# Second attention of a vision tower: in four of six score rounds, two products with the same keys become one of 392 columns

## The reference, cut to what matters

```
q = layernorm(x @ Wq.T per head) ; k = layernorm(x @ Wk.T per head) ; v = x @ Wv.T
scores = einsum('bqhs,bkhs->bhqk', q, k) / sqrt(16), causal
out = einsum('bhqk,bkhs->bqhs', softmax(scores), v) @ Wo.T + bo
```

## Time and profile before

| | us |
|---|---|
| runs | 1964.82, 1959.18, 1961.18 |
| median | 1961.18 |
| span of the profiled execution | 1907.7 |
| median less that span | 53.5 |
| TensorE busy in the span | 1666.0 (87%) |
| VectorE, ScalarE, GpSimd busy | 1201.1, 1076.6, 1162.9 |

### The profile page before, as it was taken

One profiled execution on the slowest core, in us unless ns is written; L12 is line 12 of the kernel. 1 busy time (PEld: TensorE's weight loads), 2 busy tenths in 40 slices (PEclk: granted clock), 3 DMA queues, 4 the chain that ended last, 5 costly groups with the idle time before them and its releaser, 6 DMA issues. The chain is left out here.

```text
span 1907.7 us, 45923 instructions
## 1 busy us (share of the span) xinstructions
PE 1666.0 (87%) x13765; PEld 1251.6 (66%) x13766; DVE 1201.1 (63%) x4836; ACT 1076.6 (56%) x2574; POOL 1162.9 (61%) x1108
## 2 busy tenths in 40 slices
PE   4999999995569764699999999999994999999996
PEld 2666666663447543467667677676662999998995
DVE  2899999983743002678888888888864343433442
ACT  2666666651436432467776776777751555555553
POOL 2455655531057885226776766767656687878876
PEclk8999999995569887699999999999997999999998
DMA  8989999931014433311111111211112455545553
GB/s 198 237 209 222 216 223 234 228 97 52 12 40 78 67 53 60 106 32 48 53 53 51 53 55 46 58 51 53 41 45 62 66 71 65 69 68 65 72 67 40
DMA packets 257801, 172.48 MB, mean 90 GB/s; under 512 B 25598, under 2 KB 250656, under 8 KB 257632
## 3 DMA queue, kind: packets, MB, share of 16 engines
q1 hardware_dynamic: 206432, 134.16, 28.9%
q0 software_dynamic: 50112, 35.64, 13.8%
q10 hardware_dynamic: 1088, 0.53, 0.2%
HBM read 117.64 MB, written 52.40 MB: 89 GB/s over the span
## 5 line engine op out<-in xcount | busy, mean ns | idle before, releaser
L2373 POOL DMA_INDIRECT out_dram<-r_yw,r_idx x212 | 332.5, 1568 | 94.2 <-issue 41.4
L2255 POOL DMA_INDIRECT rows_scratch<-routed_row,slot_u x256 | 254.2, 993 | 169.8 <-DVE slot_u L2194 106.7
L2438 ACT ACTIVATE r_hT<-r_p_up,r_b1T 128x256 f32<-128x256 f32 x424 | 191.6, 474 | 123.4 <-PE r_p_up L2413 120.0
L1920 ACT ACTIVATE a_probsT<-a_p_sc 98x392 f32<-98x392 f32 x384 | 170.7, 501 | 109.7 <-PE a_p_sc L1677 72.0
L2401 PEld LDWEIGHTS r_p_y<-w_all,r_hT 128*128 128x128 f32 x1696 | 224.1, 193 | 11.1
L2413 PE MATMUL r_p_up<-r_xgT,r_w1e 128*128 128x256 f32 x848 | 222.4, 386 | 9.3 <-DVE r_w1e L2453 8.7
L2401 PE MATMUL r_p_y<-w_all,r_hT 128*128 x1696 | 224.8, 276 | 0.0
L449 PE MATMUL p_embed<-pix,w_pix 96*128 96x392 f32 x512 | 209.2, 516 | 3.5 <-ACT pix L568 3.5
L2025 DVE TENSOR_REDUCE a_negmax<-a_p_max 98x2 bf16<-98x392 f32 x256 | 132.5, 559 | 61.4 <-PE a_p_max L1642 61.4
L718 POOL TENSOR_SCALAR vare<-mv 98x4 f32<-98x4 f32 x64 | 29.9, 467 | 218.3 <-DVE mv L703 199.5
L2413 PEld LDWEIGHTS r_p_up<-r_xgT,r_w1e 128*128 128x128 f32 x848 | 147.1, 194 | 22.5 <-issue 8.0
(11 more groups left out here) (377 smaller groups left out, 4171.6 us busy)
## 6 DMA issues: line engine op xcount, KB each, us to landing
img<-in_x_dram SPq DMA_DIRECT2D x192, 196.0 KB, 4.3
img<-in_x_dram SPq DMA_DIRECT2D x192, 189.0 KB, 4.5
r_xg<-rows_scratch SPq DMA_DIRECT2D x106, 130.0 KB
xn_scratch<-xn SPq DMA_DIRECT2D x32, 196.0 KB
h_scratch<-h SPq DMA_DIRECT2D x32, 196.0 KB
h<-h_scratch SPq DMA_DIRECT2D x32, 196.0 KB
h3b<-h_scratch SPq DMA_DIRECT2D x32, 196.0 KB
out_dram<-h SPq DMA_DIRECT2D x32, 196.0 KB
```

The source lines that it names most:

```text
L1920: act.activation(probsT[:, u % 2, i, :], p_sc[i % 2][:, 0:2 * PAIR], ACT.Exp).then_inc(exped, 1)
L2255: pool.indirect_dma_start(rows_dram, bass.IndirectOffsetOnAxis(ap=slot_u[:, u % ROWS, c, t:t + 1], axis=0), row[:, u % ROWS, c, t, :], Non ...
L2373: pool.indirect_dma_start(acc_dram, bass.IndirectOffsetOnAxis(ap=idx[:, (k - 3) % 4, t:t + 1], axis=0), yw[:, (k - 3) % 4, t, :], None, co ...
L2438: act.activation(hT[:, (k - 1) % 2, f, :], p_up[f][:, 0:G], ACT.Silu, bias=b1T[:, bass.ds(e * FC + f, 1)]).then_inc(act_h, 1)
```

## The change

Where the bank's two products have the same keys, the x = 0 turn makes both in one instruction pair of 392 columns: the moving operand is variant 0 and variant 1 of the same queries (two stretches of 196 columns, 392 elements apart), the output the whole bank as (x, c). The x = 1 turn makes nothing in these rounds. The rounds with m None are as before.

```diff
                                           q_var[rows, s4, var:var + 2, o:o + TILE], start=(x == 0), stop=False,
                                           skip_group_check=True)
-                            else:
+                            elif x == 0:
                                 o = m * PAIR
-                                pe.matmul(p_sc[p][:, x * PAIR:(x + 1) * PAIR], kT[rows, s4, o:o + TILE],
-                                          q_var[rows, s4, var + x, o:o + PAIR], start=(x == 0), stop=False,
-                                          skip_group_check=True)
+                                pe.matmul(p_sc[p][:, 0:LIVE * PAIR].rearrange("p (x c) -> p x c", x=LIVE),
+                                          kT[rows, s4, o:o + TILE], q_var[rows, s4, var:var + LIVE, o:o + PAIR],
+                                          start=True, stop=False, skip_group_check=True)
```

## The result

The changed kernel takes 1937.70 us (median of six runs, 1931.91 to 1942.93), the kernel before, with three more runs beside it, 1958.22 us (1953.33 to 1964.82). Ratio 0.9893, 95% interval 0.9872 to 0.9915: 20.5 us less, where 1.1 were forecast.

What follows compares the result with a forecast made beforehand. TensorE's streaming of columns was taken to bound the second attention; 0.8 us from the stream plus 0.3 us from stalls made 1.1 us less, 1961.18 to 1960.1 us, range 1956.5 to 1964.5.

Steps and rivals of the forecast that it cites:

- The median and the span: Whole kernel: runs' median is 53.5 us above the trace's span of 1907.7 and takes the same 1.1 us difference.
- two signs that were named for a wrong prediction: 392-column pass not 0.329 us, or a stage outside 780 to 1450 us differing by more than a clock stretch.
- Streams: Score passes: columns stay, two passes of 392 replace four of 196; 6 ns gained a round, 0.8 us in all.
- Weight loads: Score rounds: removed weight loads are worth nothing, since they lie beside the stream of the pass before.
- Order: Score products now all precede the maxima's wait for DVE; stalls at 822 and 1182.90 us shrink, together 0.3 us.
- What is late next: After the change, second attention: nothing new; round i = 6 still waits for ACT and DVE, which move along.
- The sum: Whole kernel: 0.8 + 0.3 = 1.1 us less, so 1960.1 us.
- Rival 1: Score rounds: every instruction has a price in series, 0.035 us a pair; 9.0 us gained, 1952 us; chance 0.03.
- Rival 2: Maxima's products start only behind the last score pass; 0.163 us a round, 21 us slower, 1981 us; chance 0.03.
- Rival 3: Round i = 6: DVE or ACT sets the beat, TensorE waits longer, stream gain gone; 1961 us; chance 0.07.
- Rival 4: Second attention: clock stretches fall differently; 7 us at the lower level is 3.4 us, either sign; no chance of its own.

Runs made afterwards that it cites:

- before_again: The kernel before, unedited, run and profiled a second time; ratio 0.9995 to the kernel before.
- order_only: Kernel before with all four 196-column score products of both banks ahead of the maxima's products in rounds with m 0 and 1, nothing merged; ratio 1.0018.
- merge_m0: Kernel before with the change only in the two rounds with m = 0 (i = 0 and 2), 128 of 256 products removed; ratio 0.9999.
- merge_m1: Kernel before with the change only in the two rounds with m = 1 (i = 8 and 10), the other 128 products removed; ratio 0.9895.
- scatter_late: Kernel before with only GpSimd's order changed: scatters 2, 3, 4 go behind the small inverse root of unit n-6; ratio 1.1154.

## Why the prediction was wrong

Step by step:

- **The median and the span.** Here it failed. "The runs' median is 53.5 us above the span, and takes the same difference" was taken for launch time. In every profile with its own time the two differ by 1.8 us. The 53.5 us were 2.7% of time for which I had no row, 50 times the gain that I was working out in nanoseconds; most of them stood in the very stage of the change (672.6 us from first to last score product in before_again, 636.9 in the first profile), and 12 us ahead of it. Of the two signs that were named for a wrong prediction, the pass of 392 columns doesn't show this, but the other one does: the stages ahead are 11 us longer in the profile of after than in the first of before (the first score product at 807.6 against 796.2), more than the 3.4 us of a clock stretch.
- **Streams.** Right: 5 ns a round measured against 6; 0.6 us in all (5 ns in each of 128 rounds). 392 columns in two stretches on 32 rows cost what the embedding's cost.
- **Weight loads.** Right: nothing.
- **Order.** Right in the first profile, wrong in the runs: the stall is met in most units, but taking it away (order_only, 1.0018) gains nothing: what round 2 wins (2 to 4 takes 2.85 us instead of 3.11), the next round loses (2.46 instead of 2.26).
- **What is late next.** "Nothing new" failed with the first step: late were TensorE's own signals in rounds 8 and 10, of which the first profile shows none. The sum had no term for them, and they are the gain: a period 0.70 us shorter than that of before_again, where 0.02 was forecast.
- **Rival 1**, a price for each instruction in series, had the right sign for a wrong reason (chance 0.03, 9.0 us). It is refuted as told: merge_m0 removes 512 instructions, for which it has 4.5 us, and gains nothing (its interval allows 3.1 us). What the instructions cost depends on what GpSimd does beside them: 62 ns each in rounds 8 and 10, 6 ns in rounds 0 and 2. The rule of the Trainium skill cited there ("TensorEngine Tiling (Array Packing)", instruction overhead, 60 cycles for each matmul) gives 3.2 us for either half of the change (an estimate from that page), and the runs do not agree: about 0 in merge_m0 (0.03 us a unit by the period), about 21 in merge_m1.
- **Rival 2** did not occur: line 1628 lies inside the rounds. **Rival 3** did not either, but its idea, that another engine gives the beat in the timed runs, was nearer than its 0.07: at round 2 TensorE waits for a late DVE in all 19 units.
- **Rival 4** priced the clock, and that is as good in before as in after (0.92 in all their runs).

What stays open: why a scatter delays TensorE's signals at all, and why it did not in the first profile, whose scatters stand at the same places and end 0.31, 1.61 and 2.87 us after round 8's start (0.31, 1.57 and 2.84 in before_again). So a scatter alone isn't enough, and what else it takes is unknown. Whether it is the issuing by GpSimd or the movement of the rows wasn't separated; leaving the scatters out would have left the next stage without its rows, and it wasn't tried. All runs are executions under the profiler, so nothing here tells whether it would be so without it.

## What to carry to other kernels

Set the profile's span against the timed runs before anything else: if they differ by more than the effect under study, the profile shows another execution, and a second one is worth more than any closer reading. Where an engine starts late and its releaser has long been done ("remote", or a wait with no work behind it), compare its start with the end of the matmul that signals it, and look at what GpSimd issues at that time. In this kernel fewer, longer matmuls were worth 0.8 us a unit beside such DMAs (merge_m1), and nothing measurable elsewhere (merge_m0). Moving the DMAs only moved the late signals, to places where waiting for them brought the clock down as well.

## What the runs showed of the hardware

- TensorE's semaphore increments came up to 2.2 us (before_again; 4.1 us in scatter_late) after the matmul's end while indirect DMAs were issued by GpSimd, and in bunches 34 ns apart once they came. Matmuls went on meanwhile. In the first profile of the same kernel none came over 50 ns late in this stage.
- They went on up to a limit: in after, issue in the second weighing stops for about 0.3 us in every unit, in 18 of 20 behind 14 of its 16 pairs of weight load and matmul. 28 instructions, the 4 of the product before and the 32 of the first weighing are 64. The Trainium skill gives TensorE a queue of 64 ("TensorE: Matmul & The Clock Gate", the table at its head), and the trace agrees with that number. That these 64 are the ones that wait is argued from the count; no record shows the queue. The second weighing in after, 1.04 us instead of 0.71:

```profile
1027.55 1.04 PE L1742 MATMUL a_p_av<-a_probsT,vals 98*32 98x196 f32 x16
```

- Matmuls in different strips of partitions start out of the program's order: the maxima at 1012.43 in after, the second score pass, which stands ahead of them in the program, at 1012.83.
